# A DLRM tower on one core: gram halves in pairs at the head of a step, and gathers held back until the grams are done

## What is computed

```
e = stack([tbl_f[ids[:, f]] for f in range(26)], axis=1)
combined = concat([dense[:, None, :], e], axis=1)            # 2048 x 27 x 128
inter = einsum('bnd,bmd->bnm', combined, combined)[:, triu]  # 351 pairs
h = concat([dense, inter, dense], axis=1)                    # 2048 x 607
h = relu(h @ W_top1 + b_top1)                                # 512
h = relu(h @ W_top2 + b_top2)                                # 256
y = h @ W_top3                                               # 1
```

## Time and profile before

| | us |
|---|---|
| median of 3 runs | 602.82 (600.51 to 607.83) |
| the profiled execution | 605.72 |
| its span, first to last instruction | 603.9 |
| granted TensorE clock, mean of the span | 0.822 |

### The profile page before, as it was taken

One profiled execution on the slowest core, in us unless ns is written; L12 is line 12 of the kernel. 1 busy time (PEld: TensorE's weight loads), 2 busy tenths in 40 slices (PEclk: granted clock), 3 DMA queues, 4 the chain that ended last, 5 costly groups with the idle time before them and its releaser, 6 DMA issues.

```text
span 603.9 us, 13994 instructions
## 1 busy us (share of the span) xinstructions
PE 433.2 (72%) x6369; PEld 389.7 (65%) x6369; DVE 263.3 (44%) x258; ACT 207.4 (34%) x313; POOL 253.8 (42%) x261
## 2 busy tenths in 40 slices
PE   3773277766788677787778778786777867787927
PEld 3672157655767667676667767675676766777827
DVE  5981035671544424535244434554154442465221
ACT  3550023443313333234222433233332333335713
POOL 7787545374423445154351644345433344500000
PEclk9886557987868788888787888896887878889978
DMA  8923113031102111031110311121111211101010
GB/s 202 243 55 104 39 32 99 21 108 37 27 25 83 45 33 41 18 92 33 27 45 16 101 34 27 37 86 47 29 26 29 85 42 33 41 7 58 4 58 1
DMA packets 21909, 32.79 MB, mean 54 GB/s; under 512 B 8030, under 2 KB 14846, under 8 KB 21850
## 3 DMA queue, kind: packets, MB, share of 16 engines
q0 software_dynamic: 8288, 16.83, 11.0%
q1 hardware_dynamic: 13562, 15.06, 8.8%
HBM read 28.24 MB, written 3.68 MB: 53 GB/s over the span
## 4 chain that ended last, share of the span: by engine, by line
PE 56%; issue 16%; DVE 12%; ACT 9%; another core or an unknown queue 6%; DMA 1%; SPq 0%; DVEq 0%
PE hot_ps L617 23%; PE gram_ps L642 11%; DVE one_hot L503 9%; PE mlp_ps L649 6%; PE transpose_ps L593 5%; PE mlp_ps L650 5%; PE mlp_ps L651 5%; ACT embed_t L424 4%; ACT embed_t L379 3%; PE hot_ids_ps L599 2%; DVE packed_lo L507 1%; DVE units L489 1%; DMA bounce<-units 1%; DMA rows<-bounce 1%
## 5 line engine op out<-in xcount | busy, mean ns | idle before, releaser
L351 POOL DMA_INDIRECT rows<-table,ids_sb x256 | 252.9, 988 | 272.9 <-PE transpose_ps L593 199.4
L617 PE MATMUL hot_ps<-one_hot,table_hi 125*128 125x256 f32 x640 | 200.2, 338 | 65.7 <-ACT embed_t L424 43.6
L503 DVE TENSOR_TENSOR one_hot<-hot_ids_ps,row_numbers_sb 125x1024 fp32r<-125x1024 f32 x160 | 192.4, 1236 | 110.9 <-PE hot_ids_ps L599 59.4
L617 PEld LDWEIGHTS hot_ps<-one_hot,table_hi 125*128 125x128 f32 x640 | 142.2, 222 | 81.3 <-DVE one_hot L503 46.0
L617 PE MATMUL hot_ps<-one_hot,table_lo 125*128 125x256 f32 x640 | 185.4, 315 | 0.0
L617 PEld LDWEIGHTS hot_ps<-one_hot,table_lo 125*128 125x128 f32 x640 | 143.5, 224 | 0.0
L642 PE MATMUL gram_ps<-embed_t 128*27 128x27 f32 x4096 | 77.3, 205 | 67.0 <-issue 66.1
L642 PEld LDWEIGHTS gram_ps<-embed_t 128*27 128x27 f32 x4096 | 58.8, 117 | 88.2 <-issue 85.3
L379 ACT COPY embed_t<-transpose_ps 128x512 f32<-128x512 f32 (+1 forms) x80 | 85.3, 1066 | 79.9 <-PE transpose_ps L593 51.1
L424 ACT COPY embed_t<-hot_ps 128x256 f32<-128x256 f32 x80 | 54.8, 684 | 148.2 <-PE hot_ps L617 82.1
L489 DVE COPY_PREDICATED units<-late_sb,gram_ps 128x208 f32<-128x208 int32 x32 | 35.1, 1098 | 121.2 <-ACT units L418 115.3
(11 more groups left out here) (49 smaller groups left out, 314.6 us busy)
## 6 DMA issues: line engine op xcount, KB each, us to landing
rows<-table,ids_sb POOLq DMA_INDIRECT x256
embed_t<-table SPq DMA_DIRECT2D x8, 448.0 KB
bounce<-units SPq DMA_DIRECT2D x8, 448.0 KB
scratch<-bounce SPq DMA_DIRECT2D x7, 378.0 KB
rows<-dense SPq DMA_DIRECT2D x16, 64.0 KB
scratch<-table SPq DMA_DIRECT2D x2, 448.0 KB
scratch<-w SPq DMA_DIRECT2D x1, 512.0 KB
scratch<-w_units SPq DMA_DIRECT2D x2, 252.0 KB
```

The lines of the kernel that those rows point to most:

```text
L351: nc.gpsimd.indirect_dma_start(rows[:, t2, f, :], None, tables[table], bass.IndirectOffsetOnAxis(ids_sb[:, slot, table:table + 1], 0)).the ...
L503: nc.vector.tensor_tensor(one_hot[:, n % RING], ids_over, numbers_over, ALU.is_equal).then_inc(one_hot_ready, 1)
L617: last = nc.tensor.matmul(hot_ps[:, 0:GROUP], table[:, k % HOT, step, :], one_hot[:, (2 * k + half) % RING, j, :], start=(step == 0 and ta ...
```

## The change

The order of the steps puts the four gram halves into two pairs at the head of each step, with one lookup (where there are any) and Q0 between them; M0 to M3 of the first step, M4 and the lookups H9 to H11 of the second come behind. The same holds for the last group's first step, without lookups. In GpSimd's queue, the gathers of a tile from its third bank on wait, once per tile, until all gram rounds of all tiles ahead of it are done. Banks 0 and 1 keep the old wait alone, and tiles 0 and 1 have no waits.

```diff
 TRANSPOSE_USES = TILES * TILE_BANKS
+GATE_BANK = 2
 MLP_USES = H1_CHUNKS + H2_CHUNKS + 1
...
 STEPS = [
-    "D0 S0 M0 G0 Q0 G1 M1 G2 Q1 W0 M2 G3 H0 M3 H1 Q2 H2 W1 H3 Q3 H4 H5 W2 Q4 H6 H7".split(),
-    "G0 H8 G1 H9 Q0 H10 G2 H11 M4 G3 H12 Q1 H13 W3 M5 H14 Q2 H15 W4 M6 H16 Q3 H17 W5 Q4 H18 H19".split(),
+    "D0 S0 G0 G1 H0 Q0 G2 G3 M0 H1 Q1 M1 H2 W0 M2 H3 M3 Q2 H4 W1 H5 Q3 H6 W2 Q4 H7".split(),
+    "G0 G1 H8 Q0 G2 G3 M4 H9 H10 Q1 M5 H11 H12 Q2 M6 H13 H14 W3 H15 Q3 H16 W4 H17 H18 W5 Q4 H19".split(),
 ]

 LAST_STEPS = [
-    "D0 S0 M0 G0 Q0 G1 M1 G2 Q1 M2 G3 M3 Q2 M4 M5 Q3 M6 Q4".split(),
+    "D0 S0 G0 G1 Q0 M0 G2 G3 M1 Q1 M2 M3 Q2 M4 M5 Q3 M6 Q4".split(),
     "G0 G1 G2 G3".split(),
 ]
...
                         pool.wait_ge(transposed, TILE_BANKS * (SLOTS * i + slot - TILES) + u + 1)
+                    if u == GATE_BANK and not first:
+
+                        pool.wait_ge(gram_ready, TILE_ROUNDS * (SLOTS * i + slot))
                     for f in gathers(u):
```

## The result

The changed kernel takes 646.36 us (median of 4 runs, 637.95 to 651.39) for 602.94 before: 1.060 times as long, with a 95% interval of 1.048 to 1.073. The forecast was 540, range 505 to 595, with 0.07 for "slower". It went the way of rival (b), and somewhat past its 615 to 635. Some executions of each kernel take 1 to 3% longer at a lower granted clock: the ratios here leave them out, but the profiles of the gate alone, of the change run again and of its pauses on the fifth chip are of such executions.

The account below looks back on a forecast made before the run. TensorE, busy 433 of 604 us, loses time in waits beside GpSimd's gathers. Groups 2 to 5 -34, group 1 -13, group 0 -21 and -1.5, groups 6 and 7 +2 each: -65 in all, 540 us, range 505 to 595.

Parts of the forecast that it names:

- rival (b): Beside lookups and MLP: from the fifth gather on TensorE stands until the run ends, 13 to 15 us a step, 615 to 635; chance 0.08.
- Part 1: Gram halves: gathers no longer run beside them, which takes away 12.1 us per group.
- rival (c): Paired gram halves: grams starve themselves, idling 2.2 us per pair with no gather near, +31 us, 571; chance 0.06.
- under 20: Sign in the new trace: TensorE's issue wait before grams falls from 66 to under 20 us.
- Part 2: Beside lookups and MLP: the 7 + 3 moved gathers cost 0.48 us each, 4.8 us back per group.
- high bound: Gathers beside lookups and MLP: first four free, 1.1 us each from the fifth on, 0.84 us averaged over 16.
- break-even: Price per gather beside lookups and MLP at which 208 gathers use up the 65 us won: 0.79 us.
- Part 3: M0 moves from before G0 to behind G3, so the dense splits run under the grams: gain 1.2 us per group.
- Part 4: GpSimd's queue: the wait for grams also holds seven gathers behind it; Q2 to Q4 barely wait, costed at nothing.
- Rival (d): Grams: gathers are not the cause, grams stumble wherever they stand; only 7 x -1.2 us remains, 597; chance 0.04.

## Why the prediction was wrong

Part 1, gathers leave the grams: right, with rival (c) on the side. Every pair from group 1 on runs with GpSimd idle. The issue wait is 29 us, not under 20: two of the pairs wait 2.2 and 2.6 us without a gather near, as (c) had it for all, and group 0's first step still meets the gathers of tile 2. The kernel without gathers waits 21 us too, with its 2 us gaps in the same two pairs and in the last step, so the sign of "under 20" asked for more than the gathers could give. Group 0's first step: 34 us forecast, 32.5 measured.

Part 2, the price of a gather beside lookups and MLP: this is the step that failed. I took 0.48 us, the mean over a run of 8 and one of 5, and let it hold for runs of 16. Runs of 16 cost 15.4 and 14.5 us, 0.93 a gather, above the high bound of 0.84 and above the break-even of 0.79 that the prediction gave. My own rows hinted at it: the run of 5 cost nothing and the run of 8 cost 4.7 us, about 1.1 us for each gather from its fifth on if the first four were free. Rival (b) made 13 to 15 us a step of that, and 14.5 to 15.4 were measured. With the measured price the sum of the prediction is 540 + 208 x (0.93 - 0.48) = 634 us, and the profiled execution took 638; 71.7 - 8.5 + 32 x 0.45 = 77.6 us a group, and groups 2 to 5 took 77.6. So this term alone turned the sign. The other terms hold to about 3 us each but one: in the last group I put the price of its nine gathers at nothing, and it came out 6.4 us longer than before, where I had 2. Against the high price I set the run of 13 in group 0, 0.32 us a gather. That reading was wrong too: group 0's second step takes 39.5 us in the changed kernel and 27.3 in the one without gathers, so a run of 16 beside lookups and weights, with no MLP, costs 0.76 a gather.

Part 3, M0 behind the grams: right. M0 waits for the dense split 2.2 us in the whole kernel, for 14.9 before, and G0 of a group waits 0.8 us.

Part 4, the gate costed at nothing: right for Q2 to Q4 in itself (TensorE's waits for rows are 2.4 us in all), wrong in what it makes: it is the gate that strings the gathers together.

Rival (d) was refuted by the kernel without gathers, and the base of part 1 confirmed. The page SBUF — State Buffer of the Trainium skill, section "SBUF: two separate sides", says that DMA ports and engine ports cannot contend with each other. The trace agrees for the plain copies (14.83 us for 14.82 without any). Beside indirect DMAs TensorE is held up all the same (30.2 us); whether any port has to do with it, no run here shows.

Not foreseen at all: that what hangs on the gathers, 140 us between 600 and 461 on one chip, is missing on others, where the kernel before takes 430 with all its gathers. On chips without the stall there was nothing for this change to win. There the changed schedule with fixed ids took 441 us beside 430 for the kernel before (one run), so it is no gain there either; the change itself was not run on such a chip.

What stays open: what passes between GpSimd's indirect DMA and TensorE's completions; why three of six chips show it, and whether it belongs to the chip or to its state at the time, since each was met only once; what decides when the stall sets in; and how the head of the kernel comes to differ by 16 us between two profiles of the same kernel.

## What to carry to other kernels

When work that disturbs an engine is moved away from one place, price it in the grouping that it will have in the new place: a wait that releases a queue all at once makes one long run out of several short ones. A mean over short runs can hide a threshold, so split such a stretch where the trouble begins and extrapolate the slope behind that point. And take away the suspected work once, entirely, before tuning its place: here that showed that 23% of the time hung on it (461 us for 600), and a second chip that all of it could be absent.

## What the runs showed of the hardware

- With indirect DMAs issued by GpSimd TensorE's completions can come late, and with plain ones of the same bytes from the same queue they don't: 646 and 665 us with 16 gathers in a row (on two chips), 463 with 16 copies and 461 with neither (on a third, where the kernel before takes 600). One fixed list of ids takes none of it away (652), nor do half the rows (681).
- The effect differs from chip to chip. On three chips the same kernel before took 600 to 617 us, on three others 430 to 433, and a run of 16 gathers takes GpSimd 15.1 us on both kinds.
- Where it shows, pauses after each bank brought the changed kernel to 0.90 of the time before, and the gate at bank 0 to 0.93. Where it doesn't, the same two cost: 1.14 and 1.02.
- When it sets in differs with what TensorE does. Beside grams it can be at once: in the kernel with the order alone the records stop 0.2 us after a first gather starts (216.95), and in the earlier trace rows 1.8 us after it (284.25 to 286.07). Beside MLP and lookups M1's copy was still on time and M2's was the first late one, 3.6 to 5.8 us after the first gather. Counted in matmul records since that gather, the three cases have 21, 44 and 33 to 52:

```profile
283.69:289.50 5.81, 5.81 (x52) 5.81 (x52) 2.97 (x5) 3.41 (x6) 4.59 (x5) 1.00 0.18 48
```

  So neither one time nor one number of instructions fits all three. This was only read from the traces; the kernel meant to test it met no chip with the stall.
